# An adaLN-style SSM convolution and quantised FFN on one core: the start-up loads, the weight roundings and the x transposes in another order

## Chip, cores, metric

The kernel runs on 1 core of one Trainium2 chip. The time is the device time of one execution in microseconds; the median of three runs is the measure.

## What is computed

x is [64, 32, 512] float32: 64 sequences, 32 channels, 512 steps. Two blocks follow each other, and the result is added to x.

```python
# block 1, per channel h: a causal convolution over time with a kernel made from SSM parameters
P = (A * dt)[:, :, None] * arange(L);  K = 2 * einsum('hn,hnl->hl', Cs, exp(P)).real   # [32, 512]
y = causal_conv(u * mask, K) + (u * mask) * D[:, None];  y = y * mask                  # mask: step < length[b]
# block 2: a feed-forward net with quantised rows and ternary weights
xq   = int4_quant(y)                             # scale of a row from mean |y|
w_q  = clip(round(w / (mean(|w|) + EPS)), -1, 1) # for gate [1376,512], up [1376,512], down [512,1376]
gate, up = xq @ wq_gate.T, xq @ wq_up.T
inter = int8_quant(up * relu(gate) ** 2)         # scale of a row from max
out = x + inter @ wq_down.T
```

## The kernel before

**Tiles.** A tile is 128 rows: one channel of the first 16 for the 64 sequences (partitions 0 to 63) and one of the last 16 (partitions 64 to 127). There are T = 16 tiles, and the main loop runs over m = 0..15. For a tile, `xt(n)` transposes x on TensorE, ScalarE's `xt_copy` takes it out of PSUM, `conv(n)` multiplies by a 512-step Toeplitz matrix (`toep`, read back by DMA from the DRAM scratch `k_back`), VectorE's `y_mask` masks, ScalarE's `y_sum` and VectorE's `y_scale` make the scale, ScalarE's `y_round` rounds, and the rounded rows are transposed (on TensorE for tiles 0 and 1, by a DMA transpose `turn_q` behind them) and clipped by `q_copy`. `products(m, c)` multiplies tile m by gate and up in three column chunks c (416, 512 and 448 wide). For each chunk ScalarE does `relu_square(c)` (2 activations) and VectorE `gated(c)` (a product and a row maximum). After chunk 2 VectorE rounds the tile into `inter_q`, which a DMA transpose on SyncE's queue turns (`it_loaded`); `down(n)` multiplies a tile by the down weight five iterations later (LAG = 5).

**Start-up.** Everything above needs two things first. The tables: VectorE computes powers of exp(A dt) from the parameters, GpSimd the rest of them, `k_sums(i)` contracts them on TensorE to a piece of the convolution kernel (`K_PARTS`: 4, 4 and 8 pairs of channels), `k_copy(i)` and `store_k(i)` put it into `k_back`, and `load_toep(n)` reads it as Toeplitz tiles. The weights: gate and up come in three parts each (`PARTS`, 1024, 1024 and 512 KB, and a left-over of 192 KB), ScalarE's `weight_sum` makes mean |w| partial sums part by part, `mean(m)` on TensorE adds them over the partitions, `weight_mean(m)` makes 1/mean on VectorE, `weight_round` (ScalarE or VectorE) scales into int16, `turn(i)` transposes 2 blocks of 128 rows on TensorE (order `TURNS`, banks `TURN_BANK`), and `weight_copy` clips to -1..1 into `gate_t` and `up_t` (`COPY_ACT`, `COPY_DVE` say which engine). The down weight has two parts (1280 and 1472 KB) with sums at the end of m = 0 and m = 1 on ScalarE, roundings in m = 2 (`down_round`), and four large DMA transposes on SyncE's queue (`turn_down(k)`, int<-int, in m = 2 and m = 3).

**Queues.** Each engine's program is written by hand and runs in order; semaphores join them. DMAs are issued by SyncE (SP), ScalarE (ACT) and GpSimd (POOL). x lies in four quads of four tiles; a quad is loaded in two halves of 64 partitions (`load_half`, 512 KB). Quad 0 comes at start, half 0 behind SP's weights and half 1 behind ACT's. Quads 1 to 3 are issued by GpSimd (`load_quad`): quad 1 behind the first table piece once up is rounded, quads 2 and 3 in m = 2 (quad 2 waits for `winv_ready` 3, quad 3 for the down roundings, since it overwrites down's raw words). The place at which VectorE holds `inter_q` until its transpose has landed is

```python
if m >= 1:
    dve.wait_ge(it_loaded[(m - 1) % IRING], 16 * ((m - 1) // IRING + 1))
```

(L1134). TensorE's order at the start is mean(0), turn(0), turn(1), k_sums(0), mean(1), xt(0), turn(2..4), xt(1), turn(5), two dummy multiplications (`keep_clock`), conv(0), ...; in an iteration it is chunk 0, chunk 1, xt(m+4), chunk 2, down, conv(m+4).

## Time and profile before

| | us |
|---|---|
| median of 3 runs | 235.47 (233.21 to 236.16) |
| the profiled execution, its own time | 233.82 |
| its span in the trace | 231.9 |
| TensorE busy | 179.8 (78%) |
| VectorE busy | 157.1 (68%) |
| ScalarE busy | 116.1 (50%) |
| GpSimd busy | 31.9 (14%) |

The span is what the trace covers; 1.9 us of the execution's own time lie around it. All positions are microseconds from the span's start. In the chain of waits each piece is followed back to what released it; the views by stretch give the busy time of each engine between two times. Where a line of the trace names a tile `raw`, `int`, `toep` or `g`, the buffer numbers are left out.

### The profile page before, as it was taken

The numbers are of one execution on the slowest core, as the hardware profiler recorded it, in microseconds if no ns is written. First come the engines' busy times: TensorE is split into PE (matmuls) and PEld (weight loads), VectorE is DVE, ScalarE is ACT, GpSimd is POOL, SyncE is SP. The second block draws the span as 40 slices with busy tenths as digits, with TensorE's granted clock in tenths as the row PEclk, the third lists the DMA queues.
The fourth block names the chain that finished last, engine by engine and source line by source line (L and its number), as shares of the span: only waits on it lengthen the run. The fifth ranks groups of instructions, "written<-read, shape, count | busy, mean of one in ns | idle before, by whom it ended". The sixth has DMA issues, their size and how long they took to land.

```text
span 231.9 us, 3341 instructions
## 1 busy us (share of the span) xinstructions
PE 179.8 (78%) x1069; PEld 95.7 (41%) x1085; DVE 157.1 (68%) x424; ACT 116.1 (50%) x191; POOL 31.9 (14%) x84
## 2 busy tenths in 40 slices
PE   1002099979798987802799999999999999999983
PEld 1002087654354543400254544545445454444442
DVE  6935337557557797007988678886777888899662
ACT  2341788265487885501262926538274462742730
POOL 8330571990000060000000000000000000000000
PEclk9999999999999999965589999999999999999998
DMA  4899709995732589999933664735557152752715
GB/s 148 293 356 215 149 5 278 344 255 179 209 41 62 127 191 155 128 144 229 205 85 113 123 154 86 188 116 110 145 103 183 39 107 50 151 103 49 153 25 113
DMA packets 48127, 34.25 MB, mean 148 GB/s; under 512 B 37134, under 2 KB 37422, under 8 KB 47982
## 3 DMA queue, kind: packets, MB, share of 16 engines
q1 hardware_dynamic: 44222, 24.60, 48.3%
q10 hardware_dynamic: 2800, 6.29, 8.5%
q0 software_dynamic: 1088, 3.15, 7.2%
q8 instruction: 9, 0.15, 0.3%
q14 instruction: 8, 0.07, 0.1%
HBM read 21.07 MB, written 4.28 MB: 109 GB/s over the span
## 4 chain that ended last, share of the span: by engine, by line
PE 63%; DMA 15%; DVE 6%; ACT 6%; SPq 5%; issue 4%; DVEq 0%; ACTq 0%
PE gate_ps L604 14%; PE up_ps L609 12%; PE down_ps L641 10%; DMA raw<-in_L_ffn_w_up_dram 10%; PE conv_ps L529 8%; DMA raw<-inter_q 5%; SPq L382 5%; PE conv_ps L641 4%; PE tr_dve_ps L529 4%; PE down_ps L529 3%; PE tr_act_ps L515 3%; ACT int L699 2%; PE gate_ps L552 1%; ACT g L768 1%; DVE inter L1091 1%
## 5 line engine op out<-in xcount | busy, mean ns | idle before, releaser
L768 ACT ACTIVATE g<-gate_ps,gu_scale 128x416 f32<-128x416 f32 (+2 forms) x48 | 30.3, 632 | 58.2 <-PE gate_ps L604 58.1
L609 PE MATMUL up_ps<-up_t,q_t 128*128 128x416 bf16 (+2 forms) x191 | 45.6, 362 | 9.6 <-DVE inter L1091 9.5
L1091 DVE SCALAR_TENSOR_TENSOR inter<-up_ps,gu_scale,g 128x416 f32<-128x416 f32 (+2 forms) x48 | 33.3, 693 | 24.6 <-ACT g L771 24.3
L604 PE MATMUL gate_ps<-gate_t,q_t 128*128 128x416 bf16 (+2 forms) x180 | 43.4, 361 | 0.6
L1095 DVE TENSOR_REDUCE imax<-inter 128x1 f32<-128x416 f32 (+2 forms) x48 | 30.3, 631 | 1.7
L609 PEld LDWEIGHTS up_ps<-up_t,q_t 128*128 128x128 bf16 x192 | 18.9, 99 | 28.7 <-DVE inter L1091 9.9
L771 ACT ACTIVATE g<-g 128x416 f32<-128x416 f32 (+2 forms) x48 | 28.1, 586 | 1.5
L641 PE MATMUL down_ps<-down_t,i_t 128*128 128x512 bf16 (+1 forms) x119 | 27.7, 379 | 0.1
L604 PEld LDWEIGHTS gate_ps<-gate_t,q_t 128*128 128x128 bf16 x192 | 17.9, 98 | 15.9 <-issue 2.6
L529 PE MATMUL conv_ps<-toep,x_t 128*64 128x512 f32 (+3 forms) x128 | 21.2, 477 | 3.6 <-ACT x_t L722 3.6
L699 ACT ACTIVATE int<-raw 128x2048 bf16<-128x2048 f32 (+3 forms) x8 | 15.6, 1944 | 14.6 <-DMA raw<-in_L_ffn_w_gate_dram 8.2
L734 ACT ACTIVATE y_int<-y,yscale 128x512 int16<-128x512 f32 x16 | 11.5, 721 | 15.6 <-DVE yscale L1027 14.2
L641 PEld LDWEIGHTS down_ps<-down_t,i_t 128*128 128x128 bf16 (+1 forms) x121 | 11.8, 98 | 13.7
L529 PEld LDWEIGHTS conv_ps<-toep,x_t 128*64 128x64 f32 x128 | 9.1, 147 | 17.4 <-issue 11.3
L1138 DVE TENSOR_SCALAR inter_q<-inter,iscale 128x1376 int16<-128x1376 f32 x15 | 14.0, 936 | 0.5
L505 PE MATMUL down_ps<-wsum,averaging 128*128 128x1 f32 x16 | 3.4, 324 | 13.8 <-ACT int L699 13.8
L726 ACT ACTIVATE y_abs<-y 128x512 bf16<-128x512 f32 x16 | 9.9, 616 | 7.0 <-DVE y L1019 7.0
L529 PE MATMUL tr_dve_ps<-toep,x_t 128*64 128x512 f32 (+3 forms) x80 | 11.9, 439 | 1.4 <-ACT x_t L722 1.4
L552 PE MATMUL up_ps<-ident_bf,int 128*128 128x128 bf16 (+1 forms) x44 | 4.9, 285 | 10.0 <-ACT int L705 9.0
L1137 DVE RECIPROCAL iscale<-gam 128x1 f32<-128x1 f32 x15 | 2.5, 163 | 14.3 <-DMA raw<-inter_q 13.8
L722 ACT COPY x_t<-tr_act_ps 128x512 f32<-128x512 f32 x16 | 9.1, 571 | 5.1 <-PE tr_act_ps L515 5.1
L641 PE MATMUL conv_ps<-down_t,i_t 128*128 128x512 bf16 (+1 forms) x44 | 10.2, 379 | 0.0
(176 smaller groups left out, 216.8 us busy)
## 6 DMA issues: line engine op xcount, KB each, us to landing
toep<-k_back SPq DMA_DIRECT2D x16, 512.0 KB, 3.9
out_dram<-o_sb SPq DMA_DIRECT2D x30, 128.0 KB, 2.4
raw<-in_x_dram POOLq DMA_DIRECT2D x6, 512.0 KB, 13.8
raw<-in_L_ffn_w_down_dram ACTq DMA_DIRECT2D x1, 1472.0 KB, 17.2
raw<-in_L_ffn_w_down_dram ACTq DMA_DIRECT2D x1, 1280.0 KB, 13.7
raw<-in_L_ffn_w_gate_dram ACTq DMA_DIRECT2D x1, 1024.0 KB, 5.7
raw<-in_L_ffn_w_gate_dram SPq DMA_DIRECT2D x1, 1024.0 KB, 12.7
raw<-in_L_ffn_w_up_dram SPq DMA_DIRECT2D x1, 1024.0 KB, 22.2
```

The source lines that it names most:

```text
L382: sp.dma_start_transpose(dn_turned[:, k], w_int[2][:, k, :]).then_inc(down_turned[k], 16)
L529: mm = pe.matmul(bank[half * B:(half + 1) * B, 0:L - i * P], x_t[n % 2][:, i, half * B:(half + 1) * B], toep[n % 4][:, half, i * P:L], sta ...
L604: mm = pe.matmul(gate_ps[bank][:, 0:cn], q_t[m % 3][:, i, :], gate_t[:, i, c0:c0 + cn], start=(i == 0), stop=(i == KB - 1))
L609: mm = pe.matmul(up_ps[bank][:, 0:cn], q_t[m % 3][:, i, :], up_t[:, i, c0:c0 + cn], start=(i == 0), stop=(i == KB - 1))
L641: mm = pe.matmul(bank[:], i_t[n % 2][0:r, c, :], down_t[0:r, c, :], start=(c == 0), stop=(c == IB - 1))
L699: nc.scalar.activation(w_bits[m][weight_part(m, i)], raw[m][weight_part(m, i)], ACT.Abs, accum_out=wsum[:, m, i:i + 1]).then_inc(w_summed, 1)
L734: nc.scalar.activation(y_int[n % 2][:], y[n % 3][:], ACT.Copy, scale=yscale[n % 2][:]).then_inc(y_rounded, 1)
L768: nc.scalar.activation(g2[bank][:, 0:cn], gate_ps[bank][:, 0:cn], ACT.Relu, scale=gu_scale[m % 4][:, 0:1]).then_inc(relu_done, 1)
L771: nc.scalar.activation(g2[bank][:, 0:cn], g2[bank][:, 0:cn], ACT.Square).then_inc(g2_ready, 1)
L1091: v.scalar_tensor_tensor(out=inter[:, c0:c0 + cn], in0=up_ps[bank][:, 0:cn], scalar=gu_scale[m % 4][:, 1:2], in1=g2[bank][:, 0:cn], op0=AL ...
L1095: return v.tensor_reduce(imax[:, c:c + 1], inter[:, c0:c0 + cn], AX.X, ALU.max, apply_absolute_value=True)
L1138: v.tensor_scalar(inter_q[:, 0:I], inter[:], iscale[:], None, ALU.mult).then_inc(inter_quant, 1)
```

## The change

**Queues.** GpSimd issues no DMA any more. The D vector goes to SP's queue ahead of its weights (and the zeroing of `d_tail` to the front of GpSimd's program, as SP waits for it); lengths and scales go to SP's queue behind x. SP now carries gate part 1, up part 0, up's left-over, x half 0; ACT gate parts 0 and 2, gate's left-over, up parts 1 and 2, x half 1. Quads 1 and 2 of x are issued in halves by SP right behind the first four Toeplitz loads, and by ACT behind y_round(0) and in m = 0. The down weight's loads, which ACT issued ahead of y_sum(0), are now issued in m = 0 behind that x half. Quad 3 is issued in m = 4.

**Start-up.** VectorE's `weight_mean(0)` stands behind the tables instead of ahead of them. VectorE rounds all of gate but part 2 (part 0 in two halves), ScalarE only gate part 2, and ScalarE does all six weight sums without a break. `mean` is one multiplication with all partial sums instead of two or three, and VectorE adds them. The turns have another order and a fifth bank, `tr_dve_ps`. `k_sums(0)` stands ahead of the turns, `k_sums(1)` in m = 0.

**Main loop.** `xt(m+4)` stands behind chunk 0 instead of chunk 1, and `xt_copy` behind `relu_square(1)` ahead of `y_round`; `xt(3)` and `xt(4)` move forward in m = 0.

TensorE's order at the start, before, up to conv(0). L505 is mean, L552 the turns, L567 k_sums(0), L515 xt, L558 keep_clock:

```order
L505 MATMUL down_ps<-wsum,averaging 128x1 x3
L552 MATMUL up_ps<-ident_bf,int 128x128 x16
L567 MATMUL tr_dve_ps<-pw,ka 40x32 x8
L505 MATMUL down_ps<-wsum,averaging 128x1 x3
L515 MATMUL tr_act_ps<-ident,x_first 128x128 x4
L552 MATMUL up_ps<-ident_bf,int 128x128 x8
L552 MATMUL gate_ps<-ident_bf,int 128x128 x16
L515 MATMUL tr_act_ps<-ident,x_first 128x128 x4
L552 MATMUL up_ps<-ident_bf,int 128x128 x8
L558 MATMUL conv_ps<-steps,ident_bf 128x512 x2
```

and now (L499 is mean, L545 the turns, L562 k_sums(0), L508 xt, L551 keep_clock):

```order
L499 MATMUL down_ps<-wsum,averaging 128x3
L562 MATMUL tr_dve_ps<-pw,ka 40x32 x8
L545 MATMUL up_ps<-ident_bf,int 128x128 x16
L499 MATMUL down_ps<-wsum,averaging 128x3
L508 MATMUL tr_act_ps<-ident,x_first 128x128 x4
L545 MATMUL gate_ps<-ident_bf,int 128x128 x8
L508 MATMUL tr_act_ps<-ident,x_first 128x128 x4
L545 MATMUL gate_ps<-ident_bf,int 128x128 x8
L545 MATMUL tr_dve_ps<-ident_bf,int 128x128 x8
L551 MATMUL conv_ps<-steps,ident_bf 128x512 x2
```

k_sums(0) is now ahead of all turns, a mean is one multiplication, and one turn fewer (5 of 12) stands ahead of conv(0).

ScalarE's order from the weight sums on, before. L699 is a sum, L705 a rounding, L722 an xt_copy:

```order
L699 ACTIVATE int,wsum<-raw 128x2048 x2
L699 ACTIVATE int,wsum<-raw 128x1536
L699 ACTIVATE int,wsum<-raw 128x2048
L705 ACTIVATE int<-raw,winv 128x2048
L699 ACTIVATE int,wsum<-raw 128x2048
L699 ACTIVATE int,wsum<-raw 128x1536
L705 ACTIVATE int<-raw,winv 128x2048
L722 COPY x_t<-tr_act_ps 128x512
```

and now (L697 a sum, L703 a rounding, L720 an xt_copy):

```order
L697 ACTIVATE int,wsum<-raw 128x2048 x2
L697 ACTIVATE int,wsum<-raw 128x1536
L697 ACTIVATE int,wsum<-raw 128x2048 x2
L697 ACTIVATE int,wsum<-raw 128x1536
L720 COPY x_t<-tr_act_ps 128x512
L703 ACTIVATE int<-raw,winv 128x1536
```

Both roundings of 2048 words have gone from ScalarE; one of 1536 has come, behind the sums and xt_copy(0).

ScalarE's order in m = 0 from relu_square(1) to the down weight's first sum (L699), before. L768 and L771 are relu_square, L726 y_sum, L734 y_round, L722 xt_copy:

```order
L768 ACTIVATE g_1<-gate_ps,gu_scale 128x512
L771 ACTIVATE g_1<-g_1 128x512
L726 ACTIVATE y_abs,ysum<-y 128x512
L768 ACTIVATE g_0<-gate_ps,gu_scale 128x448
L771 ACTIVATE g_0<-g_0 128x448
L734 ACTIVATE y_int<-y,yscale 128x512
L722 COPY x_t<-tr_act_ps 128x512 x2
L699 ACTIVATE int,wsum<-raw 128x4x640
```

and now (L762 and L765 relu_square, L720 xt_copy, L341 the second half of x's quad 2, L780 the down weight's loads, L724 y_sum, L732 y_round, L697 the sum):

```order
L762 ACTIVATE g_1<-gate_ps,gu_scale 128x512
L765 ACTIVATE g_1<-g_1 128x512
L720 COPY x_t<-tr_act_ps 128x512
L341 DMA raw<-in_x_dram 64x4x512
L780 DMA raw<-in_L_ffn_w_down_dram 128x4x640
L780 DMA raw<-in_L_ffn_w_down_dram 128x4x736
L724 ACTIVATE y_abs,ysum<-y 128x512
L762 ACTIVATE g_0<-gate_ps,gu_scale 128x448
L765 ACTIVATE g_0<-g_0 128x448
L732 ACTIVATE y_int<-y,yscale 128x512
L720 COPY x_t<-tr_act_ps 128x512
L697 ACTIVATE int,wsum<-raw 128x4x640
```

The down weight's loads now stand seven rows ahead of its first sum; before, they stood ahead of y_sum(0) in the start-up. xt_copy(3) and xt_copy(4) stand apart.

```diff
-        TURNS = (0, 1, 2, 6, 7, 3, 8, 9, 4, 10, 5, 11)
-        TURN_BANK = (0, 1, 0, 2, 3, 1, 2, 3, 1, 3, 1, 3)
-        COPY_ACT, COPY_DVE = (1, 2, 4, 5, 10), (0, 3, 6, 7, 8, 9, 11)
+        TURNS = (0, 1, 2, 6, 7, 3, 4, 8, 9, 5, 10, 11)
+        TURN_BANK = (0, 1, 2, 3, 4, 0, 1, 2, 3, 4, 1, 4)
+        COPY_ACT, COPY_DVE = (1, 2, 4, 6, 9, 11), (0, 3, 5, 7, 8, 10)
...
+            sp.wait_ge(pool_zeros, 1)
+            for g in range(2):
+                row = g * JR + JA - 1
+                sp.dma_start(d_tail[row:row + 1, :, JB - 1],
...
             load_inner(sp, 0, w_gate, 1)
             load_inner(sp, 1, w_up, 0)
-            load_inner(sp, 1, w_up, 2)
+            load_left(sp, 1, w_up)
             load_half(sp, 0, 0)
...
+            for i in range(3):
+                sp.wait_ge(w_rounded[1][i], rounds(1, i))
+            load_half(sp, 1, 0)
+            load_half(sp, 2, 0)
             store_k(1)
...
+                if m == 4:
+                    load_half(sp, 3, 0)
...
-                if i == 0:
-                    for j in range(3):
-                        pool.wait_ge(w_rounded[1][j], 1)
-                    load_quad(pool, 1)
-
-            pool.wait_ge(winv_ready, 3)
-            load_quad(pool, 2)
-            for i in range(2):
-                pool.wait_ge(w_rounded[2][i], 2)
-            load_quad(pool, 3)
...
-                for i in range(parts):
-                    mm = pe.matmul(down_ps[:, m:m + 1], averaging[:], wsum[:, m, i:i + 1],
-                                   start=(i == 0), stop=(i == parts - 1))
-                mm.then_inc(w_mean_ps, 1)
+                pe.matmul(down_ps[:, 4 * m:4 * m + parts], averaging[:], wsum[:, m, 0:parts],
+                          start=True, stop=True).then_inc(w_mean_ps, 1)
...
             for m in range(T):
                 products(m, 0)
+                if m > 0 and m + EARLY < T:
+                    xt(m + EARLY)
                 products(m, 1)
                 if m == 0:
+                    k_sums(1)
+                    xt(3)
                     conv(2)
                     first_q(1)
...
-                if m > 0 and m + EARLY < T:
-                    xt(m + EARLY)
                 products(m, 2)
                 if m == 0:
-                    xt(3)
+                    xt(EARLY)
                     conv(3)
-                    xt(EARLY)
...
             load_inner(act, 0, w_gate, 2)
+            load_left(act, 0, w_gate)
...
             load_inner(act, 1, w_up, 1)
+            load_inner(act, 1, w_up, 2)
             load_half(act, 0, 1)
...
                 relu_square(1)
                 if m == 0:
+                    xt_copy(3)
+                    for i in range(3):
+                        act.wait_ge(w_rounded[0][i], rounds(0, i))
+                    load_half(act, 2, 1)
+                    down_rows = w_down.rearrange("(c p) i -> p c i", p=P)
+                    for i in range(2):
+                        s = weight_part(2, i)
+                        act.dma_start(raw[2][s], down_rows[s]).then_inc(w_loaded[2][i], 16)
                     y_sum(2)
-                elif m + 2 < T:
+                elif m + EARLY < T:
+                    xt_copy(m + EARLY)
+                if 1 <= m < T - 2:
                     y_round(m + 2)
                 relu_square(2)
                 if m == 0:
                     y_round(2)
-                    xt_copy(3)
-                if m + EARLY < T:
-                    xt_copy(m + EARLY)
+                    xt_copy(EARLY)
+                if m == 4:
+                    for i in range(2):
+                        act.wait_ge(w_rounded[2][i], rounds(2, i))
+                    load_half(act, 3, 1)
...
-            weight_mean(0)
             scratch_u, scratch_v = inter[:, 0:128], inter[:, 128:256]
...
-            weight_copy(0)
-            dve.wait_ge(d_loaded, 32)
-            k_copy(0)
+            weight_mean(0)
+            dve.wait_ge(winv_ready, 1)
+            for c in (0, 2):
+                v.tensor_scalar(w_int[0][:, c:c + 2, :], raw[0][:, c:c + 2, :], winv[:, 0:1], None,
+                                ALU.mult).then_inc(w_rounded[0][0], 1)
+                if c == 0:
+                    dve.wait_ge(d_loaded, 32)
+                    k_copy(0)
+            weight_round(0, 1)
             weight_mean(1)
             weight_round(1, 0)
-            weight_round(0, 2)
+            weight_copy(0)
+            weight_round(1, 1)
             weight_copy(3)
-            weight_round(1, 1)
             weight_round(1, 2)
```

## Rows read from the trace of the kernel before

**Rows 1.** By stretch: length, busy of PE, PEld, DVE, ACT, POOL (instructions), PEclk, DMA share, GB/s.

```profile
49.60:64.96 15.36, 13.09 (x86) 6.49 (x84) 7.72 (x17) 9.37 (x15) 2.93 (x6) 1.00 0.76 197
64.96:75.06 10.10, 9.00 (x77) 5.01 (x77) 6.93 (x18) 7.73 (x11) 0.00 (x0) 1.00 0.19 36
75.06:84.07 9.01, 7.91 (x49) 4.24 (x49) 7.44 (x19) 8.03 (x14) 1.99 (x2) 1.00 0.63 143
84.07:93.05 8.98, 7.51 (x45) 3.80 (x45) 7.12 (x20) 5.58 (x11) 1.72 (x2) 1.00 1.13 176
93.05:116.35 23.30, 10.86 (x46) 4.39 (x45) 9.98 (x22) 5.26 (x10) 0.00 (x0) 0.67 1.05 177
116.35:126.93 10.58, 10.53 (x57) 5.10 (x56) 8.81 (x20) 5.26 (x10) 0.00 (x0) 0.93 0.40 103
```

**Rows 2.** Waits over the whole span: engine, line, released by: us, times, longest.

```profile
DVE iscale L1137 <- DMA raw<-inter_q: 13.8, 1, 13.8
```

**Rows 3.** The page's 40 slices of the span: TensorE's granted clock in tenths; DMA rate.

```profile
PEclk9999999999999999965589999999999999999998
GB/s 148 293 356 215 149 5 278 344 255 179 209 41 62 127 191 155 128 144 229 205 85 113 123 154 86 188 116 110 145 103 183 39 107 50 151 103 49 153 25 113
```

**Rows 4.** The chain that ended last: start, us, what.

```profile
2.59 22.16 DMA raw<-in_L_ffn_w_up_dram
32.08 1.44 PE down_ps L505 x6
39.63 2.30 PE conv_ps L529 x16
48.45 0.73 PE tr_dve_ps L567 x16
93.89 11.93 DMA raw<-inter_q
111.89 4.53 PE conv_ps L529 x16
```

**Rows 5.** SyncE's queue, how long single issues took: start, us, what.

```profile
82.17 11.68 SPq L382 DMA_TRANSPOSE int<-int  x2
93.89 9.85 SPq L394 DMA_TRANSPOSE raw<-inter_q  x1
105.72 4.45 SPq L382 DMA_TRANSPOSE int<-int  x2
```

**Rows 6.** DMA issues: destination, source, queue, count, KB each, median us to landing.

```profile
raw<-in_x_dram POOLq DMA_DIRECT2D x6, 512.0 KB, 13.8
raw<-in_L_ffn_w_down_dram ACTq DMA_DIRECT2D x1, 1280.0 KB, 13.7
x_first<-in_x_dram SPq DMA_DIRECT2D x1, 512.0 KB, 23.4
```

**Rows 7.** ScalarE's timeline at the start: sums of up, a rounding, the down weight's issue.

```profile
24.78 1.91 ACT L699 ACTIVATE int<-raw 128x2048 bf16<-128x2048 f32 x1 [6.43 <-DMA raw<-in_L_ffn_w_up_dram]
26.69 1.99 ACT L705 ACTIVATE int<-raw,winv 128x2048 int16<-128x2048 f32 x1
30.47 1.47 ACT L699 ACTIVATE int<-raw 128x1536 bf16<-128x1536 f32 x1
39.00 0.93 ACTq L754 DMA_DIRECT2D raw<-in_L_ffn_w_down_dram  x2
```

**Rows 8.** As rows 1, at the start: the stretch in which ScalarE's half of x flows.

```profile
18.00:23.00 5.00, 1.44 (x6) 1.35 (x6) 2.78 (x19) 0.35 (x2) 0.00 (x0) 1.00 1.02 211
```

**Rows 9.** VectorE's timeline: the weight mean of gate and the end of the tables.

```profile
19.95 0.16 DVE L974 COPY wscale<-down_ps 128x1 f32<-128x1 f32 x1 [6.07 <-PE down_ps L505]
25.08 0.22 DVE L318 TENSOR_TENSOR ka<-inter 64x64 f32<-64x64 f32 x1
```

**Rows 10.** Waits of SyncE's queue: line, released by: us, times, longest.

```profile
SPq L364 <- DMA k_back<-k_sb: 8.8, 3, 6.5
```

**Rows 11.** ScalarE's timeline, end of m = 0: the down weight's first sum.

```profile
62.49 2.34 ACT L699 ACTIVATE int<-raw 128x2560 bf16<-128x2560 f32 x1
```

98 lines of the change are left out of this document (46 added, 52 removed).

## Prediction

> **What bounds the kernel now.** I read the views in this order: the busy time by stretch, the list of waits, the granted clock, the chain that ended last, and then the queues and timelines where the chain leaves TensorE.
>
> The stretches are cut at the first product of m = 0 to 6, so each is one iteration [rows 1]. From m = 6 (126.93) on I expect nothing from the change: an iteration is then TensorE's work end to end (in m = 5 already 10.53 of 10.58 us are busy). The time to be had lies ahead of 126.93. Iterations 1 to 3 last 10.10, 9.01 and 8.98 us at 9.00, 7.91 and 7.51 busy, so TensorE idles 1.1 to 1.5 us in each. m = 0 lasts 15.36 at 13.09 busy. m = 4 lasts 23.30 at 10.86 busy, at a granted clock of 0.67 on average. That is the hole.
>
> What ends last in the hole: VectorE waits 13.8 us for a DMA transpose of inter_q [rows 2]. The clock follows: the slices (5.8 us each) from 98.6 to 116 show 6, 5 and 5 tenths, so the lower level of 1.2 GHz, after TensorE had gone idle [rows 3]. The chain has the transpose from 93.89 for 11.93 us, and behind it a convolution of 4.53 us that takes 2.30 at 39.63 [rows 4]. Why does the transpose take so long? On SyncE's queue the first two issues of down's transposes took 11.68 us together and the next transpose 9.85, while two more of down's took 4.45 at 105.72 [rows 5]. What ran beside the slow ones and not beside the fast ones is the load of x's quads 2 and 3, 2 MB issued by GpSimd in m = 2 (six such halves, median 13.8 us to landing) [rows 6]. DMA is at 1.13 and 1.05 of its engines' time there but moves only 176 GB/s [rows 1], against up to 356 in other slices [rows 3]. So the hole is a collision of those loads with the transposes.
>
> At the start the chain lies in up's load, 22.16 us from 2.59, then in ScalarE's work; mean(1) takes 1.44 from 32.08 and conv(0) starts at 39.63 [rows 4]. ScalarE waits 6.43 us for up's first part, and its last sum of up ends at 31.94 (30.47 + 1.47) [rows 7].
>
> **Term A: the start, up to the first product of m = 0.**
> *Landing.* The first three slices, to 17.4, moved 148, 293 and 356 GB/s, 4.6 MB [rows 3]; from 18.0, when ACT's half of x flows, it is 211 [rows 8], and SP's half landed 23.4 us after its issue, at about 29.7 [rows 6]. Now ACT carries 512 KB more of the weights ahead of its half of x, so almost no x flows before the weights are through. Of 5.7 MB of weights 1.1 MB are left at 17.4; at 356 that is 3.1 us, so they end at 20.5. Then x, 1 MB: two halves for different partitions at once. Between 211 and 356 I take 300: 3.5 us, with the receipt landed at about 25.
> The Trainium skill, "SBUF — State Buffer", section "Can I just issue two DMAs to hit both halves?", answers no: two transfers at partitions 0 and 64 measured only 6% over one. By that rule x would land some 1.5 us later than I say. No run here shows it yet.
> *ScalarE.* A rounding of 1.99 us stood between two of up's sums (26.69) [rows 7]; it and its twin go. Up's three sums, 1.91, 1.91 and 1.47 with some 0.2 between, take 5.5 us; the landings of their parts, by the count above 19 to 22.5, let them end at 24.8 instead of 31.9: 7.1 gained.
> *TensorE.* mean(1), six products in 1.44, becomes one of about 0.3: 1.1 gained. From its end (33.5) to conv(0) stood seven pieces in 6.1 us [rows 4]; one turn goes: 0.9, of which I take 0.4, as xt(1) waits for a copy. Sum of A: 7.1 + 1.1 + 0.4 = 8.6, conv(0) at 31.0.
> What hides the rest. VectorE waited 6.07 us for gate's mean, to 19.95, and the tables behind it ended at 25.3 [rows 9]; now they run in that wait, end at 19.0, and gate's mean is there at about 19.5. k_sums(0), which stood behind the turns of a rounding that ended at 28.7 [rows 7], ends at 20.5. The store of that piece sits behind x on SP's queue until about 25, and Toeplitz tile 0 lands at about 30, just in time: if x is late, so is it. From conv(0) to the first product it was 10.0 (39.63 to 49.60). One turn more stands there now and k_sums(1), 0.73 [rows 4], has gone; TensorE waits for turn(11), whose bank ScalarE empties behind y_sum(1). I take 10.0 again: first product at 41.0. Bounds of A: -10 (weights end 1.4 us earlier, as no small loads of GpSimd run beside them) and -5 (x late by 1.5, conv(0) at the lower clock for 2.2, GpSimd's tables, which now run beside VectorE's roundings, hold some up).
>
> **Term B: m = 0 to 3.** xt(m+4) behind chunk 0 lets ScalarE copy it before conv needs it; the idle times to be had in m = 1 to 3 are 1.1, 1.1 and 1.5 [rows 1]. Against them stand two new waits.
> *Toeplitz tile 4 in m = 0.* TensorE's work is 13.09 + 0.73 = 13.8. k_sums(1) ends at about 45, and SyncE can read the tile once store_k(1) has landed: two us at best, and up to 6.5 when DMA is full [rows 10]. The read shares DMA with the last half of quad 2 and the down weight. It lands at 47 + 7 or 8, conv(4) is due at 52.5. I take a wait of 2.6: m = 0 lasts 16.4.
> *The down weight.* It was issued at 39.0 [rows 7] and its first 1280 KB landed 13.7 us later [rows 6], at 52.7, for a sum at 62.49 [rows 11]: 9.8 us of slack. Now it is issued at about 46.5 behind 512 KB of x on its own queue, and ScalarE is at the sum at 53. I take 12.5 to landing: 59. The sum takes 2.34 + 0.2, so ScalarE is busy until 61.5, where relu_square(0) of m = 1 is due at 58.3. Behind it on ScalarE are that relu, y_sum(3), relu_square(1) and xt_copy(5), 4 us: conv(5) at 65.4, TensorE is ready at 64.1. m = 1: 9.0 + 1.3 = 10.3. In m = 2 the second, longer sum ends behind the first gate product too: 7.9 + 0.8 = 8.7; in m = 3 the down roundings do the same: 8.6.
> The starts are so 41.0, 57.4, 67.7 and 76.4, and 85.0 for m = 4, against 93.05: 8.05 gained. Term B gives 0.55 back. Bounds: 3 gained (nothing waits) and 5 lost (rival 1).
>
> **Term C: m = 4 and 5.** No x moves in m = 2 and 3. Down's transposes cost SyncE about 4.45 a pair [rows 5]; the second pair is issued by 89 and landed by 91, tile 3's inter_q transpose by 92, and VectorE wants it at 94. The wait of 13.8 goes, and the lower clock with it. What is late next is VectorE, which has down's four copies in m = 4 and is busy 9.98 and 8.81 us in m = 4 and 5 [rows 1]: TensorE waits about 2 us for it in m = 5. I take 8.4 and 11.7 against 23.30 and 10.58: 13.8 gained. Quad 3 is needed in m = 8. Bounds: 15 gained (both at TensorE's pace) and 6.
>
> **Sum.** 8.6 - 0.55 + 13.8 = 21.8 (rounded down). The profiled execution took 233.82, so 212.0; the median of the runs, 235.47, is 0.7% above it: 213.5. A measurement of this kernel tells about 2%, 4.7 us, from no change.
>
> **Rivals.**
> 1. *The down weight becomes the bound.* For: its slack of 9.8 us is gone; against: no other large load runs then. If it lands at 63, ScalarE is busy until 65.5 and TensorE waits 3.5 us in m = 1; the clock may fall as it did in the hole, and ten us of work at the lower level cost 5. 213.5 + 3.5 + 5 = 222.
> 2. *The hole only moves.* Quad 3 now meets the transposes of m = 4 and 5. For: beside x one of them took 9.85 us to issue [rows 5]. Against: 1 MB instead of 2, none of it from GpSimd, and down's transposes are through. At half of 13.8 and 2 of clock: 213.5 + 7 + 2 = 222.5.
> 3. *x's halves serialise and the clock is low in conv(0).* A is 5.5: 216.5.
> 4. *Slower.* ScalarE now issues loads in m = 0 and m = 4 in the middle of its work. An issue can stand: SyncE's stood 9.85 us [rows 5], and behind ScalarE's would stand every relu. 10 us in both places, each with 5 us of lower clock, make 30 against 21.8: 243.5. From 6 us per place it ends above before. Against: ScalarE's two issues at 39.0 took 0.93 [rows 7].
> That the loads stay on GpSimd's queue is excluded by the order.
>
> **How the numbers follow.** The forecast with 207 to 217: 0.52; rival 1 0.19, rival 2 0.15, rival 3 0.11 (inside that range), rival 4 0.03. The range takes in rivals 1 and 2: 207 to 223. Faster by over 2% (below 230.8) is all but rival 4 and 1 and 2 together: 0.93; same 0.04; slower 0.03.
>
> **What would show it.** For A, conv(0) at 30 to 32 and up's last sum ending at 24 to 26. For B, ScalarE waiting about 6 us for the down weight, and under 1.3 us of TensorE's idle time in each of m = 1 to 3. For C, no wait of VectorE over 2 us for inter_q's transpose, no 5 among the clock's slices in the middle, m = 6 starting at 105. The prediction is wrong if m = 4 still lasts over 12 us, if a wait of TensorE over 3 us stands in m = 1, or if m = 6 and later take other than 9.9 us.

## The result

| | before | changed |
|---|---|---|
| median of 4 runs | 235.72 (233.21 to 236.16) | 212.76 (212.16 to 218.25) |
| the profiled execution, its own time | 233.82 | 212.41 |
| its span | 231.9 | 210.6 |
| conv(0) starts | 39.6 | 34.5 |
| first product of m = 0 | 49.60 | 44.00 |
| first product of m = 4 | 93.05 | 85.45 |
| first product of m = 6 | 126.93 | 105.51 |

The ratio of the times is 0.904, with an interval of 0.895 to 0.912: 9.6% faster, 213.5 predicted. Of one program some runs come out a few per cent slower at a lower granted clock (218.25 is one, at 0.961), so below I compare the starts of stretches in the profiles, and times only where they differ by more than that, or between runs whose clock was granted in full (1.00). Of the 21.3 us of span, 5.6 were gained up to the first product, 2.0 in m = 0 to 3 (41.45 us long, 43.45 before), and 13.8 in m = 4 and 5 (20.06 us long, 33.88 before). From m = 6 on an iteration takes 9.87 as before.

The page, 40 slices of the span, TensorE's granted clock in tenths and the DMA rate, to be read against [rows 3]: the 6, 5 and 5 of the hole are gone.

```profile
PEclk9999999999999999999999999999999999999999
...
GB/s 107 359 384 279 151 143 260 195 104 111 362 350 140 132 140 227 157 210 254 189 163 116 133 125 120 141 123 149 102 169 77 95 50 157 39 168 66 102 52 101
```

Iterations 0 to 5 by stretch, against [rows 1] (length, busy time of PE, PEld, DVE, ACT and POOL with instructions, clock, DMA share, GB/s). m = 4 is 7.49 long at 7.49 busy; what is left over stands in m = 0 (3.0 us idle) and m = 5 (2.4).

```profile
44.00:60.78 16.78, 13.76 (x102) 7.39 (x100) 7.83 (x18) 9.25 (x15) 0.26 (x1) 1.00 0.70 223
60.78:69.72 8.94, 8.89 (x78) 5.01 (x77) 5.95 (x16) 7.53 (x13) 0.00 (x0) 1.00 0.67 169
69.72:77.35 7.63, 7.58 (x48) 4.02 (x47) 6.80 (x20) 7.33 (x13) 0.00 (x0) 1.00 0.58 134
77.35:85.45 8.10, 7.62 (x46) 3.71 (x45) 7.27 (x18) 6.69 (x12) 0.00 (x0) 1.00 0.92 199
85.45:92.94 7.49, 7.49 (x46) 3.79 (x45) 7.25 (x17) 5.38 (x10) 0.00 (x0) 1.00 1.13 203
92.94:105.51 12.57, 10.17 (x57) 4.71 (x56) 11.54 (x28) 5.38 (x10) 0.00 (x0) 1.00 0.99 222
```

SyncE's queue (start, us to issue), against [rows 5]: the first pair of down's transposes takes 3.86 and not 11.68, the transpose of inter_q behind it 1.60 and not 9.85. No wait of VectorE for inter_q is left in the list of waits, where [rows 2] had 13.8.

```profile
77.27 3.86 SPq L401 DMA_TRANSPOSE int<-int  x2
81.17 1.60 SPq L413 DMA_TRANSPOSE raw<-inter_q  x1
...
86.08 4.38 SPq L401 DMA_TRANSPOSE int<-int  x2
90.50 1.73 SPq L413 DMA_TRANSPOSE raw<-inter_q  x1
```

The chain that ended last, against [rows 4]. It still starts in up's load, and has two new pieces: 2.97 us before conv(4), which no engine released (TensorE waits there for Toeplitz tile 4, whose read left at 49.79 and took 8.6 us to land), and VectorE's copies of the down weight.

```profile
4.13 19.97 DMA raw<-in_L_ffn_w_up_dram
...
25.94 3.55 ACT int L697 x5
...
55.50 2.97 issue
...
90.80 1.58 DVE down_t L1012 x2
```

ScalarE's timeline, against [rows 7] and [rows 11]. It waits for gate's part 1 until 15.37, then 5.28 us for up's part 0. Its last sum of up ends at 29.4 (31.9 before). Its first sum of the down weight starts at 58.77, after 4.09.

```profile
15.37 1.91 ACT L697 ACTIVATE int<-raw 128x2048 bf16<-128x2048 f32 x1 [5.98 <-DMA raw<-in_L_ffn_w_gate_dram]
...
24.12 1.91 ACT L697 ACTIVATE int<-raw 128x2048 bf16<-128x2048 f32 x1 [5.28 <-DMA raw<-in_L_ffn_w_up_dram]
...
27.92 1.47 ACT L697 ACTIVATE int<-raw 128x1536 bf16<-128x1536 f32 x1
...
58.77 2.34 ACT L697 ACTIVATE int<-raw 128x2560 bf16<-128x2560 f32 x1 [4.09 <-DMA raw<-in_L_ffn_w_down_dram]
```

The landings of the start, us from issue, against [rows 6]. Up's part on ACT's queue (part 1) had landed by 16, its part 0 on SP's queue, issued at 4.13, only at 24.1, while ScalarE had been free since 18.8.

```profile
raw<-in_L_ffn_w_up_dram ACTq DMA_DIRECT2D x1, 1024.0 KB, 12.6
...
raw<-in_L_ffn_w_up_dram SPq DMA_DIRECT2D x1, 1024.0 KB, 20.0
...
x_first<-in_x_dram ACTq DMA_DIRECT2D x1, 512.0 KB, 17.6
x_first<-in_x_dram SPq DMA_DIRECT2D x1, 512.0 KB, 21.0
```

TensorE's waits with their line (us in total, times, longest): the 3.0 before conv(4) and the 2.2 in m = 5.

```profile
PE conv_ps L522 <- issue: 3.0, 1, 3.0
PE up_ps L604 <- DVE inter L1101: 2.8, 3, 2.2
```

### The profile page after: what moved, and what is told of

The parts are those of the page before. It is cut to its first block, busy times and chain, and to the rows that moved or that the text cites. A ratio compares the mean times of both kernels' runs of the same rounds, so it can differ in the third digit from the quotient of the medians.

```text
span 210.6 us, 3324 instructions
## 1 busy us (share of the span) xinstructions
PE 172.7 (82%) x1059; PEld 91.9 (44%) x1075; DVE 159.1 (76%) x425; ACT 114.1 (54%) x191; POOL 28.3 (13%) x71
## 4 chain that ended last, share of the span: by engine, by line
PE 66%; DMA 11%; DVE 9%; issue 5%; ACT 5%; SPq 2%; DVEq 0%; ACTq 0%
PE gate_ps L599 15%; PE up_ps L604 14%; PE down_ps L636 11%; DMA raw<-in_L_ffn_w_up_dram 9%; PE conv_ps L522 7%; PE tr_dve_ps L522 5%; PE conv_ps L636 3%; PE tr_act_ps L508 3%; PE down_ps L522 3%; DVE inter L1101 2%; DMA out_dram<-o_sb 2%; ACT int L697 2%; DVE y L1025 1%; DVE imax L1105 1%; ACT g L762 1%
## 5 line engine op out<-in xcount | busy, mean ns | idle before, releaser
L762 ACT ACTIVATE g<-gate_ps,gu_scale 128x416 f32<-128x416 f32 (+2 forms) x48 | 30.6, 637 | 49.7 <-PE gate_ps L599 49.3
L604 PE MATMUL up_ps<-up_t,q_t 128*128 128x512 bf16 (+2 forms) x190 | 44.6, 357 | 2.9 <-DVE inter L1101 2.8
L599 PE MATMUL gate_ps<-gate_t,q_t 128*128 128x448 bf16 (+2 forms) x181 | 42.8, 356 | 0.6
L765 ACT ACTIVATE g<-g 128x416 f32<-128x416 f32 (+2 forms) x48 | 28.1, 586 | 1.5
L604 PEld LDWEIGHTS up_ps<-up_t,q_t 128*128 128x128 bf16 x192 | 18.5, 98 | 22.0 <-DVE inter L1101 4.1
L697 ACT ACTIVATE int<-raw 128x2048 bf16<-128x2048 f32 (+3 forms) x8 | 15.5, 1942 | 18.0 <-DMA raw<-in_L_ffn_w_gate_dram 8.7
L522 PE MATMUL conv_ps<-toep,x_t 128*64 128x512 f32 (+3 forms) x128 | 19.0, 439 | 3.0 <-issue 3.0
L499 PE MATMUL down_ps<-wsum,averaging 128*128 128x3 f32 (+1 forms) x6 | 1.5, 313 | 20.7 <-ACT int L697 20.7
L732 ACT ACTIVATE y_int<-y,yscale 128x512 int16<-128x512 f32 x16 | 11.6, 722 | 6.0 <-DVE yscale L1033 5.7
L724 ACT ACTIVATE y_abs<-y 128x512 bf16<-128x512 f32 x16 | 9.9, 616 | 5.3 <-DVE y L1025 5.3
L499 PEld LDWEIGHTS down_ps<-wsum,averaging 128*128 128x128 f32 x6 | 1.4, 272 | 21.2 <-ACT int L697 21.1
L720 ACT COPY x_t<-tr_act_ps 128x512 f32<-128x512 f32 x16 | 9.2, 573 | 2.5 <-PE tr_act_ps L508 2.5
L1025 DVE SCALAR_TENSOR_TENSOR y<-steps,lens,conv_ps 128x512 f32<-128x512 f32 x8 | 5.9, 743 | 6.0 <-PE conv_ps L522 6.0
## 6 DMA issues: line engine op xcount, KB each, us to landing
raw<-in_L_ffn_w_down_dram ACTq DMA_DIRECT2D x1, 1472.0 KB, 12.8
raw<-in_L_ffn_w_up_dram ACTq DMA_DIRECT2D x1, 1024.0 KB, 12.6
```

The costliest lines, as they stand in the source:

```text
L522: mm = pe.matmul(bank[half * B:(half + 1) * B, 0:L - i * P], x_t[n % 2][:, i, half * B:(half + 1) * B], toep[n % 4][:, half, i * P:L], sta ...
L599: mm = pe.matmul(gate_ps[bank][:, 0:cn], q_t[m % 3][:, i, :], gate_t[:, i, c0:c0 + cn], start=(i == 0), stop=(i == KB - 1))
L604: mm = pe.matmul(up_ps[bank][:, 0:cn], q_t[m % 3][:, i, :], up_t[:, i, c0:c0 + cn], start=(i == 0), stop=(i == KB - 1))
L697: nc.scalar.activation(w_bits[m][weight_part(m, i)], raw[m][weight_part(m, i)], ACT.Abs, accum_out=wsum[:, m, i:i + 1]).then_inc(w_summed, 1)
L724: nc.scalar.activation(y_abs[:], y[n % 3][:], ACT.Abs, accum_out=ysum[n % 2][:]).then_inc(y_summed, 1)
L732: nc.scalar.activation(y_int[n % 2][:], y[n % 3][:], ACT.Copy, scale=yscale[n % 2][:]).then_inc(y_rounded, 1)
```

## The experiments

Each experiment is an edit of the changed kernel, but one (b_quads_time). The changed kernel, run again beside them (ctl), took 212.29 with the clock granted in full, and 216.17 to 216.99 in three runs at a mean of 0.984 or 0.992.

### The hole: the moment or the queue?

**a_pool_m2.** Quads 2 and 3 go back to where and by whom they were loaded before:

```diff
-            load_half(sp, 2, 0)
...
+            pool.wait_ge(winv_ready, 3)
+            for half in range(2):
+                load_half(pool, 2, half)
+            for i in range(2):
+                pool.wait_ge(w_rounded[2][i], 2)
+            for half in range(2):
+                load_half(pool, 3, half)
...
-                    load_half(act, 2, 1)
```

(quad 3's halves in m = 4 go as well.)

> The changed kernel, with quads 2 and 3 of x again loaded by GpSimd behind the down weight's mean and rounding (in m=2 and 3, as in the kernel before); all else as changed. Theory (the two quads on the down weight's transposes made the hole in m=4): the issue of the second pair of transposes takes about 10 to 12 us again where the changed kernel has 3.9 and 4.4, VectorE waits about 14 us for a transpose of inter_q, and the time is 225 to 228. Rival (the hole went because of the new front or the other order of work): 211 to 214.

Measured: 226.69 (225.88 to 228.18). The first pair of down's transposes took 11.40 us to issue, the next transpose 7.15, and VectorE waited:

```profile
DVE iscale L1149 <- DMA raw<-inter_q: 12.2, 1, 12.2
```

m = 4 lasted 22.38 at a granted clock of 0.69, m = 5 9.87: 32.25 for the two, against 20.06. That is 12.2 of the 13.8 us of term C, from this one part. The rest of the change stayed: m = 4 started at 89.05 (in ctl at 89.85).

**a_act_m2.** The same moment with ScalarE's hardware queue: both halves of quad 2 behind `winv_ready` 3, both of quad 3 behind the down roundings.

```diff
                 if m == 2:
+                    act.wait_ge(winv_ready, 3)
+                    for half in range(2):
+                        load_half(act, 2, half)
                     down_round(2)
                     down_round(3)
+                    for i in range(2):
+                        act.wait_ge(w_rounded[2][i], 2)
+                    for half in range(2):
+                        load_half(act, 3, half)
```

> The same moment, another queue: the changed kernel with quads 2 and 3 loaded in m=2 by ScalarE's hardware queue, four halves around its two roundings of the down weight. Theory T (any 1 MB of x's narrow rows behind the transposes makes the hole, whatever queue carries it): transposes issued in 10 to 12 us, hole of some 14 us, 224 to 228. Theory Q (GpSimd's queue made it): transposes issued in about 4 us, 211.5 to 214.

Measured: 226.28 (223.73 to 226.58), within 0.4 of the kernel with GpSimd's loads. The pair took 11.83 us, the transpose behind it 8.41:

```profile
78.05 11.83 SPq L400 DMA_TRANSPOSE int<-int  x2
89.92 8.41 SPq L412 DMA_TRANSPOSE raw<-inter_q  x1
```

m = 4 and m = 5 by stretch, columns as above: 30.83 together, the clock again low.

```profile
88.27:107.31 19.04, 9.01 (x46) 4.01 (x45) 7.94 (x19) 5.38 (x10) 0.00 (x0) 0.73 1.15 175
107.31:119.10 11.79, 10.04 (x57) 4.79 (x56) 10.44 (x26) 5.38 (x10) 0.00 (x0) 1.00 0.56 147
```

m = 3, in which ScalarE issues the four halves (2.6 us on its queue), took 10.14 and not 8.10, so the loss from m = 3 to 5 is 12.8 us; with GpSimd's loads, where m = 3 stayed at 8.10, it is 12.2. Theory Q has fallen: the hole doesn't need GpSimd's queue. The Trainium skill, "DMA: Bandwidth & Descriptors", section "Issuing engines are not separate DMA queues", says that transfers of all issuing engines run on the same 16 DMA engines and interleave; by that rule the two kernels should show much the same hole, and they do (12.2 and 10.8 us in m = 4 and 5 over the changed kernel's 20.06).

**b_quads_time.** The other way round, one part alone in the kernel before. GpSimd keeps its queue, and quad 2 follows quad 1, quad 3 comes in m = 5:

```diff
                     load_quad(pool, 1)
+                    load_quad(pool, 2)
 
-            pool.wait_ge(winv_ready, 3)
-            load_quad(pool, 2)
             for i in range(2):
                 pool.wait_ge(w_rounded[2][i], 2)
+            pool.wait_ge(inter_quant, 5)
             load_quad(pool, 3)
```

> One part alone: the kernel before, with GpSimd's quad 2 issued right behind quad 1 and its quad 3 once m=4 has been quantized; the queue is as before. Theory T (the moment is what matters): the hole in m=4 of 14 us goes and little of it comes back with quad 3 in m=5: 221 to 223 against 235.5. Theory Q (GpSimd's queue beside any transpose is slow): quad 3 beside m=5's transposes makes a hole of its own, 226 to 236.

Measured: 223.37 (220.89 to 225.66) against 233.31 for the kernel before, run beside it. m = 4 and 5 took 8.77 and 10.32, 19.09 together against 33.88: 14.8 gained, the pairs of transposes took 3.43 and 4.30 us. It paid elsewhere: m = 0 lasted 19.69 (15.36), since TensorE now waited 3.49 us for Toeplitz tile 4 and then ran conv(4) in 3.88 us at a lower clock (2.37 before). The little store that the tile's read waits for left at 47.25, beside quad 2, and the read could leave only at 58.83 (49.52 and 56.40 before); the tile itself landed in 4.3. m = 6 lasted 10.90 (9.87) beside quad 3. So the moment is what counts, and the loads had a price where they went too: 5.4 us in m = 0 and 6, against the 14.8.

### The front: why up's part 0 was late

Three edits, with the control.

**a_order.** ScalarE sums up's parts as 1, 2, 0.

```diff
...
+            for i in (1, 2, 0):
+                weight_sum(1, i)
```

> The changed kernel, with ScalarE's three sums of up taken as parts 1, 2, 0 and not 0, 1, 2. In the changed kernel ScalarE stood from 18.8 to 24.1 us for up's part 0 (SP's queue) while parts 1 and 2 (its own queue) had landed by about 16 and 19.5. Theory (the late part of SP's queue sets the front, the order of the sums decides how much of it is on the path): parts 1 and 2 are summed from about 18.8 to 22.4, part 0 from 24.1 to 26.2, the sums end 3.2 us sooner than 29.4, conv(0) starts about 2.5 to 3.2 sooner (31.3 to 32 against 34.5), and the time falls to about 209.5 to 210.5. Rival (x or the filter's tile is as late as the sums): conv(0) gains under 1 us, the time stays at 212 to 213.

Measured: 215.88 (214.04 to 216.10). The sums ended at 28.4, only 1.0 sooner, because part 2 waited until 25.05: its left-over of 192 KB stands behind part 0 on SP's queue, which I had overlooked.

```profile
25.05 1.48 ACT L697 ACTIVATE int<-raw 128x1536 bf16<-128x1536 f32 x1 [4.29 <-DMA raw<-in_L_ffn_w_up_dram]
```

And conv(0) started at 34.46, no sooner at all: the turns between were slower (below, in the section on the hardware). The edit tells nothing for or against the late queue.

**f_x_late.** ScalarE's half of x_first is issued behind its sums of gate in the program.

```diff
             load_inner(act, 1, w_up, 2)
-            load_half(act, 0, 1)
...
+            for i in range(3):
+                weight_sum(0, i)
+            load_half(act, 0, 1)
...
```

> The changed kernel, with ScalarE's half of x_first issued behind its sums of gate (about 19) instead of at 4.93. Theory X (that half, on the queue that ran out of weights at 18.5, took the transfers that up's part 0 on SP's queue still needed): part 0 lands at 21 to 21.5 instead of 24.1, up's sums end at 26.5 to 27 instead of 29.4, conv(0) at 32 to 32.5, time about 210.5. Theory S (SP's queue is late because its rows began only at 9.5, behind the two loads of D): part 0 still lands after 23.5, time 212 to 213. Rival to both: x itself lands past 27 and nothing is won.

Measured: part 0 was there at 21.0, up's sums ended at 26.3, conv(0) started at 31.54 and the first product at 41.01. ScalarE's timeline (the issue left the queue at 15.34, ahead of the sum's end):

```profile
15.34 0.54 ACTq L341 DMA_DIRECT2D x_first<-in_x_dram  x1
...
21.01 1.91 ACT L696 ACTIVATE int<-raw 128x2048 bf16<-128x2048 f32 x1 [2.32 <-DMA raw<-in_L_ffn_w_up_dram]
...
24.81 1.47 ACT L696 ACTIVATE int<-raw 128x1536 bf16<-128x1536 f32 x1
```

As theory X had it, 3 us were won at the front. The time, though, was 212.48 (211.92 to 212.84): in the profiled run m = 0 lasted 19.06 and m = 1 9.57 (16.78 and 8.94), the granted clock was 0.50 from 55.6 to 60, behind a wait of 3.09 us before conv(4), and m = 4 started at 85.37, where the changed kernel's does. All four runs had a clock of 0.984 or 0.992.

**f_d_mid.** On SP's queue gate's part 1 goes ahead of the two loads of D.

```diff
+            load_inner(sp, 0, w_gate, 1)
             sp.wait_ge(pool_zeros, 1)
             for g in range(2):
...
-            load_inner(sp, 0, w_gate, 1)
             load_inner(sp, 1, w_up, 0)
```

> The changed kernel, with gate's part 1 issued ahead of the two loads of D on SP's queue (up's part 0 behind them as before). Theory X: SP's rows begin near 6.5, gate's part 1 lands 2 to 3 us sooner (ScalarE's sum of it starts at 12.5 to 13.5 and not 15.4), but the transfers were full in this stretch, so up's part 0 still lands at 23.5 to 24.2 and conv(0) stays within 0.5 of 34.5. Theory S: part 0 lands 2 to 3 us sooner with it, conv(0) near 32, time near 210.

Measured: 211.03 (207.96 to 213.01; 207.96 was the one with the clock granted in full, against 212.29 of ctl). Part 0, issued at 3.96, landed 16.7 us later:

```profile
raw<-in_L_ffn_w_gate_dram SPq DMA_DIRECT2D x1, 1024.0 KB, 10.6
...
raw<-in_L_ffn_w_up_dram SPq DMA_DIRECT2D x1, 1024.0 KB, 16.7
```

and ScalarE's sums stood 2.6 and 3.4 us sooner than in the changed kernel, conv(0) at 31.08, the first product at 40.55:

```profile
12.73 1.91 ACT L697 ACTIVATE int<-raw 128x2048 bf16<-128x2048 f32 x1 [3.39 <-DMA raw<-in_L_ffn_w_gate_dram]
...
20.68 1.91 ACT L697 ACTIVATE int<-raw 128x2048 bf16<-128x2048 f32 x1 [4.48 <-DMA raw<-in_L_ffn_w_up_dram]
...
24.48 1.47 ACT L697 ACTIVATE int<-raw 128x1536 bf16<-128x1536 f32 x1
```

In the profiled run only 0.9 of the 3.4 us were left at m = 6 (104.58 against 105.51): the wait before conv(4) was 3.81, and m = 5 took 14.25 and not 12.57, with the clock at 0.50 behind its wait of 2.18.

So theory S was right about its edit, and my expectation by theory X (part 0 stays late) wrong; yet X's own edit won the same 3 us. Both are halves of one cause. The KB whose single DMA packets had ended by a time, counted in the three traces:

```
us from the start            10    14    17    18    20    22    24
changed, SP's weights       252   998  1562  1686  1786  2176  2240   of 2240
f_d_mid, SP's weights       728  1360  1938  2104  2230  2240  2240
f_x_late, SP's weights      278  1022  1592  1914  2232  2240  2240
changed, ACT's half of x      0     0     0    88   424   512   512   of 512
f_d_mid, ACT's half of x      0     0     0     0    16   216   480
f_x_late, ACT's half of x     0     0     0     0     0   200   512
```

In the changed kernel SP's weight rows begin at 8.1, behind the loads of D, and at 6.1 with gate's part 1 ahead of them; ACT's queue alone moves weights until then, so the total rate is full and nothing seems lost. But from then on the two queues move about the same (746 and 758 KB from 10 to 14), ACT's 3264 KB end at about 18.5, and its half of x follows from 16.9 on. From 17 to 20 SP's queue moved 224 KB, where it moved 564 in the three us before; in f_x_late, with no half of x on ACT's queue, it moved 640. It is not only x's own 424 KB that took the place: all transfers together fell from 386 GB/s (14 to 17) to 257. The packets of x are of 8 KB and those of the weights of 2 KB; whether that sets the shares no run separates. Start SP's rows sooner, or start x later: either way ACT's half of x no longer flows beside the last of the weights.

### The middle: Toeplitz tile 4, the down weight and the x turns

**g_down_sp.** SP issues both loads of the down weight, right behind `load_toep(4)`; ScalarE's are gone.

```diff
             store_k(1)
             load_toep(4)
...
+            for i in range(2):
+                s = weight_part(2, i)
+                sp.dma_start(raw[2][s], down_rows[s]).then_inc(w_loaded[2][i], 16)
...
```

> The changed kernel, with the two loads of the down weight issued by SP behind the filter's tile 4 instead of by ScalarE at 49.4, ahead of it. In the changed kernel TensorE stood 2.97 us before conv(4), whose tile took 8.6 us to land. Theory (the tile shared the transfers with 2.7 MB of the down weight): the tile lands in 4 to 5 us, the wait before conv(4) is under 0.5, m=0 takes 13.8 to 14.3 instead of 16.8, ScalarE's first down sum starts near 60 and delays nothing that TensorE needs by over 0.5, and the time falls by 2.3 to 3. Rival (conv(4) waits for something else, or the sum of part 0 comes so late that m=1 grows by as much): within 1 of the changed kernel.

Measured: 214.11 (212.49 to 214.70). The tile landed in 6.7 us, the wait before conv(4) fell from 2.97 to 1.08, and m = 0 lasted 14.89. But m = 1 and 2 lasted 9.67 and 8.58 (8.94 and 7.63), with waits of 0.66 and 0.88 before conv(5) and conv(6), and from the first product to m = 4 it was 40.85 against 41.45. The direction within m = 0 was right, the size not: most came back, and in the time nothing is left (the fastest run took 212.49, at 0.996; the front of the profiled one was 1.3 us late).

**i_down_early.** The down weight is issued behind ScalarE's half of quad 1, at 41.4, so that it is through before tile 4.

```diff
             load_half(act, 1, 1)
...
+            for i in range(2):
+                s = weight_part(2, i)
+                act.dma_start(raw[2][s], down_rows[s]).then_inc(w_loaded[2][i], 16)
             y_sum(1)
...
```

> The changed kernel, with the down weight's two loads issued by ScalarE behind its half of quad 1 (about 40) instead of at 49.4; quad 2's halves stay. Theory: 2.7 MB have landed by about 50, so the filter's tile 4 (issued 49.8) comes in about 4 us, TensorE's 2.97 us before conv(4) fall under 0.5 and ScalarE's 4.09 us for the down weight go too; the issue costs ScalarE under 1 us before chunk 0. m=0 takes 13.8 to 14.5 and not 16.8, starts of m=1 on 2.3 to 3 us sooner, time 209.5 to 210.5 in runs without a lower clock. Rival (the down weight now takes the transfers of quad 1 or of the filter's tiles 1 to 3): the wait moves to x(4)'s turn or to conv(1) to conv(3), and the time is within 1 of the changed kernel.

Measured: 217.19 (214.67 to 217.71). ScalarE's wait for the down weight went, and TensorE's stayed at 3.00. SyncE's queue shows why: the little store of the filter's second piece took 6.4 us to land and not 1.4, and the read of tile 4 left at 56.13; it landed in 3.7.

```profile
49.77 0.31 SPq L373 DMA_DIRECT2D k_back<-k_sb  x1
56.13 0.37 SPq L379 DMA_DIRECT2D toep<-k_back  x1
```

So taking away ScalarE's 4.09 us gained nothing, and the chain store, landing, read is what TensorE waits for. Which transfer held the store (the down weight, or SP's halves of quads 1 and 2 slowed by it) I did not separate.

**h_xt_back.** `xt(m + 4)` behind chunk 1 and its copy behind chunk 2's squares, as before, for m of 1 and more.

```diff
                 products(m, 0)
-                if m > 0 and m + EARLY < T:
-                    xt(m + EARLY)
                 products(m, 1)
...
+                if m > 0 and m + EARLY < T:
+                    xt(m + EARLY)
                 products(m, 2)
...
```

> The changed kernel, with x's turn for the tile after next put back behind chunk 1, and ScalarE's copy of it behind chunk 2's squares, in m=1 to 11 (m=0 stays). Theory (the turn behind chunk 0 took away TensorE's waits of about 1.05 to 1.4 us ahead of conv(5), (6) and (7) in the kernel before): these waits are back, m=1 to 3 take 1 to 1.4 longer each (8.9, 7.6 and 8.1 now), m=4 starts 3 to 4 later, and the time is 215 to 216.5. Rival (the order of the weights alone gave m=1 to 3 what they gained): under 1 us slower.

Measured: 217.23; the two runs with the clock in full took 214.79 and 216.38, against 212.29. TensorE's timeline has waits like those of the kernel before again, ahead of conv(5) to conv(8):

```profile
71.66 2.38 PE L522 MATMUL down_ps<-toep,x_t 128*64 128x512 f32 x16 [1.05 <-ACT x_t L720]
...
80.45 2.37 PE L522 MATMUL conv_ps<-toep,x_t 128*64 128x512 f32 x16 [1.05 <-ACT x_t L720]
...
89.77 2.37 PE L522 MATMUL tr_dve_ps<-toep,x_t 128*64 128x512 f32 x16 [1.76 <-ACT x_t L720]
...
98.55 1.72 PE L522 MATMUL conv_ps<-toep,x_t 128*64 128x512 f32 x8 [1.21 <-ACT x_t L720]
```

m = 1 to 4 lasted 10.27, 8.78, 9.33 and 8.78, 5.0 us longer together, but m = 5 only 10.31 and not 12.57. So the turn behind chunk 0 gains 5.0 and hands 2.3 back in m = 5, where TensorE waits 2.19 us for VectorE in the changed kernel. (m = 4 started 6.6 us later and not 3 to 4, since this run also waited 4.34 us before conv(4).)

**j_copy_act.** Two of VectorE's four copies of the turned down weight go to ScalarE, at the end of m = 4.

```diff
+            def down_copy(k):
+                act.wait_ge(down_turned[k], 16)
+                nc.scalar.activation(down_t[:, :, k * P:(k + 1) * P], dn_turned[:, k],
+                                     ACT.Sign).then_inc(down_copied, 1)
...
+                if m == LAG - 1:
+                    down_copy(2)
+                    down_copy(3)
...
-                if m == LAG - 1:
-                    down_copy(2)
-                    down_copy(3)
```

> The changed kernel, with two of the four limiting copies of the turned down weight given by VectorE (0.83 each) to ScalarE at the end of m=4. Theory (VectorE's copies are what TensorE waits 2.19 for in m=5): m=5 takes 10.2 to 11 and not 12.57, the time falls by 1.5 to 2.2. Rival (ScalarE's two copies, of some 1.4 each, hold back chunk 0's squares in m=5, and the wait only changes its name): within 0.7 of the changed kernel.

Measured: m = 5 lasted 10.97, 1.6 less; the wait fell from 2.19 to 0.93. The run with the clock in full took 209.79 against 212.29. ScalarE's two copies took 2.64, and chunk 0's squares began only behind them, at 98.31. The chain of the 0.93 us that are left runs through the copies, so the rival's mechanism was there too, at a smaller price than the gain.

```profile
101.31 0.93 PE L604 MATMUL up_ps<-up_t,q_t 128*128 128x448 bf16 x4 [0.93 <-DVE inter L1109]
```

**ctl.**

> The changed kernel as it is, once more, beside the three that follow: 212 to 213, conv(0) at 34.5, m=1 at 60.8, m=6 at 105.5. If a stretch of lower clock falls somewhere by chance, as one did in the run with parts 1, 2, 0 (m=0 longer by 1.7), it shows here how often.

Measured: 216.39 (212.29 to 216.99). conv(0) and the first product of the profiled run came 1.0 us later than in the changed kernel; m = 0 took 19.65 and m = 1 9.44. It is read in the section on the hardware.

### One kernel that beats both

**best.** f_d_mid and j_copy_act together, and k_sums(1) behind chunk 0 of m = 0, with VectorE's copy of it ahead of its gating:

```diff
                 products(m, 0)
+                if m == 0:
+                    k_sums(1)
...
                 products(m, 1)
                 if m == 0:
-                    k_sums(1)
                     xt(3)
...
+                if m == 0:
+                    k_copy(1)
                 gated(0)
-                if m == 0:
-                    k_copy(1)
```

> Three edits in one kernel on top of the changed one: gate's part 1 ahead of D's two loads on SP's queue (-3.4 where it was alone), the two limiting copies on ScalarE at the end of m=4 (-1.6 where it was alone), and the products for the filter's second third put behind chunk 0 of m=0 with their copy ahead of VectorE's gating, so that the filter's tile 4 is asked for about 1.5 us ahead of the down weight and not 0.4 behind it. Theory (the tile's place ahead of the down weight decides, as the load on SP's queue did in part): TensorE waits under 1 us before conv(4) (2.97 before) and stays busy enough that the lower clock behind that wait goes; first product near 40.6, m=1 at 55 to 55.8, m=6 at 98 to 99.5, span of the profiled run 202.5 to 204.5, time 204 to 206.5. Rival (the tile's 0.5 MB shares the queues with the halves of quads 1 and 2 anyway): the wait is still 2 to 3 us, and the time is 206.5 to 208.5.

Measured: 204.94 (203.18 to 206.23, 6 runs), 0.877 of the kernel before, run beside it (0.872 to 0.881). The read of tile 4 was issued at 45.60, 1.3 ahead of the down weight, and TensorE did not wait for it: m = 0 is 13.55 long at 13.55 busy. The landing of that read in the changed kernel, and in this one:

```profile
DMA to landing us min/median/max: 8.6/8.6/8.6
...
DMA to landing us min/median/max: 4.0/4.0/4.0
```

m = 0, 1, 2 and 5 by stretch:

```profile
41.53:55.08 13.55, 13.55 (x103) 7.21 (x100) 7.82 (x18) 7.21 (x14) 2.65 (x6) 1.00 0.64 179
55.08:64.57 9.49, 9.01 (x78) 5.00 (x77) 4.87 (x12) 8.09 (x13) 0.00 (x0) 1.00 0.91 280
64.57:73.54 8.97, 7.70 (x48) 4.22 (x47) 8.40 (x23) 8.88 (x14) 0.00 (x0) 1.00 0.67 129
...
88.53:99.45 10.92, 10.04 (x57) 4.79 (x56) 9.62 (x26) 7.63 (x12) 0.00 (x0) 1.00 1.09 237
```

f_d_mid alone, with the read 0.4 behind the down weight, had the tile land in 9.4 us and a wait of 3.81, and the copies on ScalarE come only in m = 4: so it is the new place of k_sums(1) that took the wait away. Two things are in it. The read leaves 4.07 us behind the first product and not 5.79, and it lands in half the time, ahead of the down weight and not behind it (6.7 in g_down_sp, ahead of it too). What was saved comes partly back, as in g_down_sp: m = 1 is 0.5 longer and m = 2 1.3 (8.94 and 7.63), the latter with 1.27 us before conv(6).

## Why the prediction was right

The time was met (213.5, measured 212.8) and the largest term with its mechanism; the sum behind it less well. Two terms missed by 3.0 and 2.6 us with opposite signs, and that they cancel was luck. Of the signs that I had named, those of A failed (conv(0) at 34.5 and not 30 to 32, up's sums ending at 29.4 and not 24 to 26); those of B and C held, but for ScalarE's wait for the down weight, 4.09 us and not 6.

- **Term C held.** 13.8 predicted and measured; m = 4 and 5 took 7.5 and 12.6 (8.4 and 11.7), and VectorE's copies were late next, as said (2.19 us in m = 5). The mechanism, x beside the transposes, is shown by a_pool_m2, a_act_m2 and b_quads_time, in both directions. "None of it from GpSimd", an argument against rival 2, was worth nothing: ScalarE's queue makes the same hole.
- **Term A was too large by 3.0.** 8.6 predicted, 5.6 measured. The step that failed is the landing: "ACT carries 512 KB more of the weights ahead of its half of x, so almost no x flows before the weights are through". I had counted bytes in total and taken the two queues to end together. SP's queue started its weight rows 5.2 us behind ACT's (8.1 and 2.9), ran out 5.3 us later (23.9 and 18.5), and x filled the gap. Up's part 0 landed at 24.1 and not about 19, the sums ended at 29.4 and not 24.8. That step alone was 4.6 us short (2.5 gained at the sums' end and not 7.1). The stretch from there to conv(0) gave 1.1 back (5.1 us and not 6.2) and that from conv(0) to the first product 0.5 (9.5 and not 10.0). Where the queues were evened out (f_d_mid) conv(0) stood at 31.08 and the first product at 40.55, against 31.0 and 41.0 predicted.
- **Term B was off by 2.6 the other way.** It was to lose 0.55 and gained 2.0. The wait for Toeplitz tile 4 came as said (2.97, 2.6 said), though I had taken two us for a store's landing "at best" where [rows 10] leave 2.3 for two of them, and it was 1.42. The step that failed is ScalarE's lateness: the waits that I had put into m = 1 to 3 (10.3, 8.7, 8.6) weren't there (8.94, 7.63, 8.10). The down weight landed in 9.3 us and not 12.5. With the late front its sum began at 58.77 all the same (59 said), but m = 1 only at 60.78. The late front isn't what hid it: in f_d_mid, with the front as early as predicted, the sum began at 56.75, m = 1 at 58.17, and m = 1 to 3 took the same 8.94, 7.63 and 8.10. In best, where m = 1 began at 55.08 and the sum at 56.39, m = 1 and 2 take 9.49 and 8.97: only with the wait for tile 4 gone too does the sum come late. h_xt_back shows that the x turn brought the gain: with it put back, m = 1 to 3 take 28.38 (24.67, and 28.09 before).
- **Rival 1** (the down weight becomes the bound) fell: m = 1 lasted 8.94 at 8.89 busy, and taking away ScalarE's wait for it saved nothing (i_down_early). **Rival 2** fell: the transposes issued from 92.33 on, as quad 3's halves left (92.17 and 94.52), took 1.2 to 1.5 us each. **Rival 3** had the size of A (5.5) but not its cause, and no low clock in conv(0). **Rival 4** fell: ScalarE's issues took 0.6 for a half of x and 1.3 for the down weight's two. In a_act_m2, where it issues four halves around its roundings, m = 3 did grow by 2.0 us.

The rule of the Trainium skill ("SBUF — State Buffer", "Can I just issue two DMAs to hit both halves?", that two transfers for the two halves serialise) can now be weighed, though no run here has one half alone. In f_x_late and f_d_mid the two halves of x_first had landed 4.2 and 5.0 us after up's part 0 (its 192 KB left-over a little before them, at 22.8 and 23.6). I had 3.5, and 5.0 by the rule. From 20 to 22 us, with both halves in flight and the weights all but through, all transfers together moved 253 and 240 GB/s, where I had taken 300 and the weights had moved at 388 and 384 (14 to 17): the measurements lean to the rule.
